# The third group of the first layer as four 64x64 quadrant matmuls, and three ReLUs instead of four

## The reference

```
x = x + conv_block(layernorm_c(x))        # 3x3 conv on 12 channels, 1x1 conv 48 -> 254,
                                          # 8x8 rfft2 * fft_w, irfft2, gelu(a) * b, 1x1 conv 127 -> 48
t = tokens(x)                             # (4, 16384, 48)
n = layernorm_t(t)
h = relu(qacc(qacc(q8(n) @ q8(W1).T) + q8(b1)))   # 48 -> 192;  q8: 5 exponent bits, 2 of mantissa
y = qacc(qacc(q8(h) @ q8(W2).T) + q8(b2))         # 192 -> 48;  qacc: 5 exponent bits, 10 of mantissa
x = from_tokens(t + y)
```

## Time and profile before

| | |
|---|---|
| median of three runs | 700.97 us |
| span of the profiled execution | 699.4 us |
| PE busy | 666.5 us (95%) |
| DVE busy | 597.9 us (85%) |
| ACT busy | 536.8 us (77%) |
| POOL busy | 456.9 us (65%) |
| mean DMA rate | 115 GB/s |

### The profile page before, as it was taken

How to read it: one execution, slowest core, us unless ns; L and a number is a source line. 1 busy time by engine, 2 the same in 40 slices (tenths; PEclk the granted TensorE clock), 3 DMA queues, 4 the chain that set the end, 5 groups by cost and what they waited for, 6 DMA issues and landing times.

```text
span 699.4 us, 19176 instructions
## 1 busy us (share of the span) xinstructions
PE 666.5 (95%) x6620; PEld 529.3 (76%) x6620; DVE 597.9 (85%) x1159; ACT 536.8 (77%) x1087; POOL 456.9 (65%) x347
## 2 busy tenths in 40 slices
PE   4879999999999999999999999999999999999984
PEld 4657877778778877787878877787788777887751
DVE  7637889988988899988988899889888999877877
ACT  4244568888888888888889888888888888877784
POOL 2605677767777777677776877677777876753353
PEclk9989999999999999999999999999999999999995
DMA  4434445444544554445444544545445543342102
GB/s 102 79 78 118 121 113 131 112 126 128 142 120 118 142 140 121 114 120 138 127 123 131 139 131 107 132 121 144 121 116 144 139 129 103 100 119 87 47 23 68
DMA packets 52207, 80.73 MB, mean 115 GB/s; under 512 B 20823, under 2 KB 36079, under 8 KB 52111
## 3 DMA queue, kind: packets, MB, share of 16 engines
q1 hardware_dynamic: 50031, 78.56, 43.2%
q10 hardware_dynamic: 2080, 0.94, 0.6%
HBM read 63.17 MB, written 16.30 MB: 114 GB/s over the span
## 4 chain that ended last, share of the span: by engine, by line
PE 87%; DVE 3%; DMA 3%; issue 2%; ACT 1%; SPq 1%; POOL 1%; DVEq 0%; ACTq 0%; POOLq 0%
PE inva L532 17%; PE invb L539 15%; PE mixp L519 13%; PE misc L548 8%; PE misc L803 8%; PE misc L619 4%; PE misc L519 4%; PE misc L663 3%; PE misc L784 3%; PE misc L568 2%; PE misc L577 2%; PE misc L653 2%; PE mixp L632 2%; PE mixp L639 2%; DMA xin<-in_x_dram 1%
## 5 line engine op out<-in xcount | busy, mean ns | idle before, releaser
L1555 POOL TENSOR_TENSOR st<-st,neg_half 128x16 f32<-128x16 f32 x32 | 93.3, 2915 | 129.2 <-DVE st L1459 129.2
L532 PEld LDWEIGHTS inva<-inv,gmix 128*127 128x127 f32 x1024 | 123.4, 191 | 25.3 <-issue 16.6
L532 PE MATMUL inva<-inv,gmix 128*127 128x128 f32 x1024 | 141.0, 281 | 0.6 <-DVE gmix L1234 0.6
L1234 DVE TENSOR_TENSOR gmix<-mixp,freq_w 128x508 f32<-128x508 f32 x192 | 122.6, 680 | 16.9 <-PE mixp L519 16.9
L539 PE MATMUL invb<-inv,gmix 128*127 128x128 f32 x1024 | 134.7, 274 | 0.1
L539 PEld LDWEIGHTS invb<-inv,gmix 128*127 128x127 f32 x1024 | 126.2, 191 | 2.1 <-DVE hbuf L1245 0.5
L897 ACT ACTIVATE hid<-misc 128x512 f16<-128x512 f32 x180 | 94.1, 599 | 17.7 <-PE misc L619 17.7
L1245 DVE TENSOR_TENSOR hbuf<-gact,invb 127x512 f32<-127x512 f32 x128 | 87.4, 683 | 22.2 <-ACT gact L889 17.7
L1584 POOL TENSOR_TENSOR st<-st,neg_half 128x16 f32<-128x16 f32 x31 | 95.4, 3077 | 16.4 <-DVE st L1313 15.9
L906 ACT ACTIVATE hid<-hid 128x512 fp8e5<-128x512 f16 x174 | 93.2, 619 | 0.0
L889 ACT ACTIVATE gact<-inva 127x512 f32<-127x512 f32 x128 | 77.5, 605 | 19.9 <-PE inva L532 19.3
(11 more groups left out here) (184 smaller groups left out, 1358.2 us busy)
## 6 DMA issues: line engine op xcount, KB each, us to landing
taps<-cz_scratch SPq DMA_DIRECT2D x63, 292.2 KB
xin<-in_x_dram SPq DMA_DIRECT2D x64, 192.0 KB, 3.3
xres<-in_x_dram SPq DMA_DIRECT2D x64, 192.0 KB, 4.1
out_dram<-ob SPq DMA_DIRECT2D x60, 192.0 KB, 2.6
taps<-cz_scratch SPq DMA_DIRECT2D x63, 146.1 KB
crm<-rm_scratch SPq DMA_DIRECT2D x58, 96.0 KB
cx<-in_x_dram SPq DMA_DIRECT2D x32, 96.0 KB
cz_scratch<-cz SPq DMA_DIRECT2D x63, 48.8 KB
```

Source lines behind the costliest of these rows:

```text
L532: mm = pe.matmul(inva[0:HID, q * PX:(q + 1) * PX], gmix[:, s % 2, q, 0:HID], inv[:], start=True, stop=True, skip_group_check=True)
L1234: dve.tensor_tensor(gmix[:, s % 2, 2 * q:2 * q + 2, 0:HID2], pair[q][:, 0:2 * HID2].rearrange("p (e c) -> p e c", e=2), freq_w[:], ALU.mul ...
L1555: pool.tensor_tensor(st1[:, 6, :], st1[:, 5, :], neg_half[:], ALU.pow).then_inc(pow1, 1)
```

## The change

The third group of both quarters and both halves becomes four matmuls of 48 rows and 64 output columns (`hidden_rest`): half j reads partitions 64j, quarter c writes output partitions 64c, half 1 goes to bank 3 and half 0 to bank 2. So one bank holds both quarters of one half, and not both halves of one quarter. The order of the six tiles in `hid16` and `hid8` is now: half 0 and 1 of quarter 0, rest of half 1, rest of half 0, half 0 and 1 of quarter 1. The ReLUs are three of 1024 elements. The second layer's products with the rest take each half's tile and the weight rows of quarter c. On PE the four quadrant matmuls stand after both parts of `inverse(t, 3, 1)`; `rows` of steps 3 to 5 stands behind them. `stream` waits for the copy out of bank 3. On ACT the order becomes: copies 0 and 1, gelu, copies 2 and 3, `convs`, copies 4 and 5. The drain at the end keeps the old layout for its last two steps and has its counts adapted.

```diff
--- before.py
+++ after.py
@@ -560,6 +560,8 @@
                 if live(t, 0):
                     pe.wait_ge(rmT_ready, a + 1 if a > 2 else 1)
+                if live(t, 5):
+                    pe.wait_ge(hid16_ready, 6 * at(t, 5) + 3)
                 pe.wait_ge(col_in, upto(64 * (c + 1)))
...
@@ -609,15 +611,34 @@
                 else:
                     pe.wait_ge(gmix_ready, upto(8 * n + 2))
                     pe.wait_ge(y16_ready, upto(2 * at(t, 6) + 2))
+                if live(t, 5) and a < ROWS_EARLY:
+                    pe.wait_ge(hid16_ready, 6 * at(t, 5) + 3)
                 dst = bank[3] if a < ROWS_EARLY else mixp[0]
                 pe.transpose(dst[0:32, 0:128], rm[:].rearrange("p a j i -> p (a j i)"), eye[:])\
                   .then_inc(rmT_done, 1)
 
+            def hidden_rest(t):
+
+                for c in range(2):
+                    for j in (1, 0):
+                        r0 = HALF * j
+                        mm = pe.matmul(bank[2 + j][HALF * c:HALF * c + HALF, :], l1h[r0:r0 + CH, 2, r0:r0 + HALF],
+                                       q16[r0:r0 + CH, 4 * c:4 * c + 4, :], start=True, stop=True,
+                                       skip_group_check=True)
+                        if c == 1:
+                            mm.then_inc(hid_done, 1)
+
             def hidden(t, c, g, dst):
 
                 r0, r1 = ((0, CH), (HALF, SPAN), (0, SPAN))[g]
                 pe.matmul(dst[:], l1h[r0:r1, g, :], q16[r0:r1, 4 * c:4 * c + 4, :], start=True, stop=True,
                           skip_group_check=True).then_inc(hid_done, 1)
+
+            def rest_product(dst, c, j):
+
+                r0, o = HALF * c, HALF * j
+                return pe.matmul(dst[o:o + HALF, :], l2[:, 2, r0:r0 + HALF], hid8[:, (3, 2)[j], :],
+                                 start=False, stop=True, skip_group_check=True)
 
             def second_layer(t):
 
@@ -627,17 +648,16 @@
                 pe.wait_ge(hid8_ready, upto(6 * l + 5))
                 pe.sem_inc(pe_held, 1)
                 for c in range(2):
-                    for g in range(2):
-                        r0 = HALF * g
-                        pe.matmul(pair[c][r0:r0 + HALF, :], l2[:, g, r0:r0 + HALF], hid8[:, 3 * c + g, :],
-                                  start=True, stop=False, skip_group_check=True)
-                for c in range(2):
                     if c == 1:
                         pe.wait_ge(hid8_ready, upto(6 * l + 6))
                         pe.sem_inc(pe_held, 1)
-                    for r0 in (0, HALF):
-                        mm = pe.matmul(pair[c][r0:r0 + HALF, :], l2[:, 2, r0:r0 + HALF], hid8[:, 3 * c + 2, :],
-                                       start=False, stop=True, skip_group_check=True)
+                    for g in range(2):
+                        r0 = HALF * g
+                        pe.matmul(pair[c][r0:r0 + HALF, :], l2[:, g, r0:r0 + HALF], hid8[:, 4 * c + g, :],
+                                  start=True, stop=False, skip_group_check=True)
+                for c in range(2):
+                    for j in range(2):
+                        mm = rest_product(pair[c], c, j)
                     mm.then_inc(y_done, 1)
 
             def turn_tokens(t):
@@ -704,11 +733,12 @@
...
                 def between():
-                    pe.wait_ge(hid8_ready, 6 * OLDER + 3)
-                    second_layer_half(0, mixp[0])
+                    pe.wait_ge(hid8_ready, 6 * OLDER + 4)
+                    older_half(0, mixp[0])
...
@@ -781,6 +811,8 @@
                     for i in range(PAIRS):
+                        if i == 4 and not peeled:
+                            pe.wait_ge(hid16_ready, upto(6 * l + 6))
...
@@ -844,17 +876,13 @@
                     hidden(t, 0, 0, bank[0])
                     hidden(t, 0, 1, bank[1])
 
-                def last_group():
-                    if live(t, 0) and 3 <= a < ROWS_EARLY:
-                        rows(t, 0)
-                    if live(t, 5):
-                        pe.wait_ge(tsq_ready, upto(2 * m + 1, 2 * STEPS))
-                        hidden(t, 0, 2, bank[2])
-
-                if live(t, 3):
-                    inverse(t, 3, 1, last_group)
-                else:
-                    last_group()
+                if live(t, 3):
+                    inverse(t, 3, 1)
+                if live(t, 5):
+                    pe.wait_ge(tsq_ready, upto(2 * m + 2, 2 * STEPS))
+                    hidden_rest(t)
+                if live(t, 0) and 3 <= a < ROWS_EARLY:
+                    rows(t, 0)
                 if a == 2:
                     keep_busy(16, bank[1])
                 if live(t, 2):
@@ -867,8 +895,6 @@
                     pe.wait_ge(hid16_ready, upto(6 * k + 2))
                     hidden(t, 1, 0, bank[0])
                     hidden(t, 1, 1, bank[1])
-                    pe.wait_ge(hid16_ready, upto(6 * k + 3))
-                    hidden(t, 1, 2, bank[2])
                 if live(t, 2):
                     convolve(t)
                     if peeled and a == 2:
@@ -888,22 +914,22 @@
                 act.wait_ge(h_ready, upto(4 * n + s - 1))
                 act.activation(gact[:, s % 2], inva[0:HID, :], ACT.Gelu).then_inc(gelu_ready, 1)
 
-            def accumulators(t, c, groups):
+            def accumulators(t, groups):
 
                 k = at(t, 5)
                 for g in groups:
-                    act.wait_ge(hid_done, upto(6 * k + 3 * c + g + 1))
-                    act.wait_ge(hid8_ready, upto(6 * (k - 1) + 3 * c + g + 1))
-                    act.activation(hid16[:, 3 * c + g, :], bank[g][:], ACT.Copy).then_inc(hid16_ready, 1)
+                    act.wait_ge(hid_done, upto(6 * k + g + 1))
+                    act.wait_ge(hid8_ready, upto(6 * (k - 1) + g + 1))
+                    act.activation(hid16[:, g, :], bank[(0, 1, 3, 2, 0, 1)[g]][:], ACT.Copy).then_inc(hid16_ready, 1)
...
@@ -1101,20 +1126,20 @@
                 if live(t, 4):
                     rest(t)
                 if live(t, 5):
-                    accumulators(t, 0, (0,))
+                    accumulators(t, (0, 1))
+                if live(t, 3):
+                    gelu(t, 3, 1)
+                if live(t, 5):
+                    accumulators(t, (2, 3))
                 if live(t, 0) and 3 <= a < ROWS_EARLY:
                     rows(t, 0)
-                if live(t, 5):
-                    accumulators(t, 0, (1, 2))
-                if live(t, 3):
-                    gelu(t, 3, 1)
                 if live(t, 2):
                     c = at(t, 2)
                     act.wait_ge(stream_done, upto(c + 1))
                     act.activation(convs[:].rearrange("p u x -> p (u x)"), bank[3][:], ACT.Copy)\
                        .then_inc(convs_ready, 1)
                 if live(t, 5):
-                    accumulators(t, 1, range(3))
+                    accumulators(t, (4, 5))
                 if live(t, 2):
                     act.wait_ge(conv_done, upto(c + 1))
                     dst = halves(zpix[:, ring(t, 2)])[:, :, 0:2 * CC].rearrange("p (g u) c -> p g u c", u=4)
@@ -1267,14 +1292,12 @@
                 order = lambda i: st1s[:, ring(t, behind, 8), i, :].rearrange("p (i j) -> p j i", j=2)
                 dve.tensor_tensor(rm[:, 1], order(6), order(2), ALU.mult).then_inc(mr_ready, 1)
 
-            def relu(t, c, parts=((0, 2), (2, 1))):
+            def relu(t, i):
 
                 k = at(t, 5)
-                for g, size in parts:
-                    dve.wait_ge(hid16_ready, upto(6 * k + 3 * c + g + size))
-                    buf = hid16[:, 3 * c + g:3 * c + g + size, :]
-                    dve.tensor_scalar(buf, buf, bq[:, g // 2:g // 2 + 1], 0.0, ALU.add, ALU.max)\
-                       .then_inc(relu_ready, size)
+                dve.wait_ge(hid16_ready, upto(6 * k + 2 * i + 2))
+                buf = hid16[:, 2 * i:2 * i + 2, :]
+                dve.tensor_scalar(buf, buf, bq[:, i % 2:i % 2 + 1], 0.0, ALU.add, ALU.max).then_inc(relu_ready, 2)
 
             def scale_tokens(t):
 
@@ -1492,6 +1515,7 @@
                     weigh(t, 3)
                 if live(t, 5):
                     relu(t, 1)
+                    relu(t, 2)
                 if live(t, 3):
                     gate(t, 3, 2)
                 if isinstance(a, int) and a == 4:
```

More of the change, by code:

```diff
@@ L692, in first_layer, with older_half @@
                         hidden(t, c, g, dst[g])
+                def older_half(c, dst):
+                    for g in range(2):
+                        r0 = HALF * g
+                        pe.matmul(dst[r0:r0 + HALF, :], l2[:, g, r0:r0 + HALF], hid8[:, 4 * c + g, :],
+                                  start=True, stop=False, skip_group_check=True)
+                    for j in range(2):
+                        mm = rest_product(dst, c, j)
+                    mm.then_inc(y_done, 1)
                 def second_layer_half(c, dst):
@@ L706, in drain @@
                 pe.wait_ge(h_ready, 4 * NEW + 2)
```

(30 more changed lines are left out.)

## The result

| | before | after |
|---|---|---|
| median of six runs | 700.86 us | 731.86 us |
| span of the profiled execution | 699.4 us | 732.7 us |

The change makes the kernel slower by a factor of 1.0449 (95% interval 1.0427 to 1.0470), 31 us. The forecast was 724 in a range of 716 to 731: the direction and the mechanism of the steady step hold, the size is outside the range. The profiled execution of the kernel after is the slowest of its six (735.15 us; the others take 728.95 to 733.09), so its span is some 3 us longer than that of a median one.

What follows compares the result with a forecast made beforehand. PE's chain was taken as the bound: 28 steps x 0.73 = 20.4 us, plus 1.5 (step 5) and 1.3 (step 3), is 23.2; with the span of 699.4 and 1.6 around it, 724.2 us, range 716 to 731.

Steps and rivals of the forecast that it cites:

- The bound: Steady steps: each lasts 19.78 us, all PE work without any wait, so any added wait counts 28 times.
- PE's own work: Steady step without any wait: two matmuls saved, nearly eaten by added changes of tile shape, -0.04 us in sum.
- rival of quadrants in pairs: Quadrant matmuls run two by two, not four at once: +6.4 us, 730.6; chance 0.09, in pairs or singly.
- The wait of `stream`: Steady step: stream loads 0.90 us later, behind ACT's copy of bank 3; the step's sum is +0.73 us.
- the wake-up: Steady step, from the end of ACT's copy to PE's first weight load for stream: 0.05 us, upper bound 0.14.
- The first steps: Step 3's later rm transpose shifts the program by 1.3 us; step 4 adds nothing; step 5 adds 1.5.
- rival on the clock: Idle pauses of about 0.7 in 20 us lower PE's clock; over 900 us at half speed half the time; chance 0.01.
- Step 5: Start, with rows also in bank 3: 0.8 us more than the steady wait, +1.5 us.
- DVE: Every step: four ReLUs become three, 0.2 us less, on an engine with no part in the steady chain.
- The drain: End of the kernel: a fourth conversion of 0.54 us in one place, costed at 0 with 0.5 as the bound.

Runs made afterwards that it cites:

- e4: The changed kernel without half 1's two quadrant matmuls, so nothing of the first layer is in bank 3 and stream waits for no copy: 706.0 us.
- e9: e1 with stream's wait for the copy written first among its waits (the built program lists them in another order): 722.38 us.
- e7: The changed kernel with twelve extra identity matmuls keeping PE busy ahead of step 4's stream: 730.19 us, ratio 1.0405.
- e2: The changed kernel with stream's wait for the copy written as the last of its waits, behind that for the taps: 727.26 us.
- e3: The changed kernel with one more ACT copy of bank 3 ahead of the copy that stream waits for: 748.26 us.
- e5: e1 with mix(t, 3) moved ahead of stream and the convolution's transposes between the two parts of inverse(t, 3, 2): 703.79 us, ratio 1.0038.
- e1: The changed kernel with rm's transpose in steps 3 to 5 back between inva and invb, its ACT copy ahead of the gelu: 726.44 us, ratio 1.0363.
- e8: The kernel before, with only rm's transpose of steps 3 to 5 moved behind invb: 705.45 us, ratio 1.0052.

## Why the prediction was right in kind and too small

- **The bound** (PE's chain, no wait to give back): right. The 28 steady steps take 25.9 us more, 0.93 each, and with the wait gone (e4) the step is within 0.06 of before.
- **PE's own work**: right. Forecast -0.04, measured -0.06 in e4. The four quadrants run at once: their four weight loads fill 0.11 us together and their matmuls 0.40 ahead of a wait and 0.34 ahead of `mix`, forecast 0.35; `convolve` takes 0.59, as forecast. The rival of quadrants in pairs did not come about.
- **The wait of `stream`**: the first step that failed; the term was there and mis-sized. Pieces after sum to 0.89 + 0.40 + 0.59 + 0.25 + 0.65 + 0.98 + 0.22 + 0.59 = 4.57, before to 3.65, +0.92 against +0.73. The one term far off is the wake-up, "From there to PE's first weight load I take 0.05", which measured 0.25 in most steps and 0.34 in a few. I had put its upper bound at 0.14, from a wait of another kind, and did not price the other waits in front of the same matmul; 0.04 is right when the late wait is the last (e9). Two smaller misses cancel, by luck: the quadrants took 0.40 for 0.35, and ACT's copy 0.59 for the 0.64 between their end and its own. Over the steady steps 25.9 us stand against the forecast 20.4: 5.5 of the 10.1 us by which the loss between the spans, 33.3, is above the forecast 23.2.
- **The first steps**: the other step that failed. Forecast +2.8 in all, with step 5's wait; measured +7.7. I moved the DMA chain by 1.3 and let the rest shift with it. In the profiled execution the chain started 1.4 later (`rm_t` at 58.76, before 57.34), but step 4's `stream` came 3.3 later; and what I did not ask is what the longer pause would do to the clock, a term that I put at nothing. It cost 2.85 by the trace of the change, and e7, without the fall, was 2 to 3 us faster. I had a rival on the clock, but only for the short pauses in every step, where the clock did stay at 1.00 and which cost nothing of the kind.
- **Step 5**: forecast +1.5, of which +1.7 falls ahead of `stream` and -0.17 behind it; 104.56 - 87.66 = 16.90 against 96.81 - 81.49 = 15.32 is +1.6, right in the profiled execution. That step 6 could wait for the taps behind it, as it does in e2, e3, e4 and e7, I had not seen.
- **DVE**: one ReLU less for a step, and no effect on the end; right. Its saving is less than forecast, since a ReLU of 1024 now takes 554 ns on average, before 481:

```profile
L1300 DVE TENSOR_SCALAR hid<-hid,bq 128x1024 f16<-128x1024 f16 x90 | 47.3, 554 | 0.0
```

- **The drain**: forecast 0, measured -0.4.
- The Trainium skill, "TensorEngine Tiling (Array Packing)", section Performance Considerations, warned that behind packed matmuls the copy out of PSUM may become the bottleneck. The runs agree in a narrower sense: ACT had the time for the copy, and only its place directly ahead of a matmul into the same bank made it a bound (e5 against e1).

What stays open: why the DMA chain of the start came back 1.9 us later than its own delay explains in the profiled execution. The traces say where: from the issue of the read back of `rm`'s factors (L415) to POOL's first product it took 67.09 - 61.57 = 5.52, before 64.03 - 60.15 = 3.88. This stretch is 3.8 to 3.9 in e1, e2, e3, e7 and e9, 4.77 in e4 and 4.89 in e8. It is long only with the late transpose, but not always then, and no run shows what decides it. So of the two theories of the start both have a part: the late transpose is the cause, and how much it costs varies with a DMA. Open is also why the changed kernel's runs spread from 728.95 to 735.15, where those before spread by 1.5; the mean granted clock is 0.985 in the fastest and 0.976 in the slowest, but only the slowest has a trace.

## What to carry to other kernels

When an engine is the whole chain, price an edit by what it puts directly ahead of the next use of the same bank: here a saved matmul of 0.22 us put a copy of 0.59 and its wake-up in front of PE, while the same edit with other PE work in between costs 0.1. Of several waits ahead of one instruction, the one that ends last should be the last to be taken, and the built program tells which that is. A small delay ahead of a pause must be followed into the clock: the chain started 1.4 us later, PE stood idle for 3.16 us and not 0.96, and the half speed behind this cost 2.85, twice the delay.

## What the runs showed of the hardware

- Each instruction of waits that PE still takes behind the late one costs some 0.1 us, and the waits stand two to an instruction: gaps of 0.25, 0.14 and 0.04 with two, one and none (the change, e2, e9).
- Four 48-row by 64-column matmuls of 512 columns in two banks run at once: 0.34 to 0.40 us with their change of shape, where the two of one half, in different columns, take 0.33 (e4).
- At step 4 the granted clock fell to 0.50 after 3.16 us of idle PE (the change), 2.92 (e4), 2.82 (e8) and 2.19 (e3), and not after 1.66 (e2) or with the idle time filled (e7); idle pauses of 0.9 in every step left it at 1.00. The length of the pause alone does not decide: at step 6 it stayed at 1.00 after 2.53 in e2 and fell after 1.88 in e3.
